# Expert weights kept in float32 and loaded in place, with the expert bias added by VectorE

## The reference, cut to what matters

```python
xk = x_prev + (x - x_prev) * tmk            # xv, xr likewise
k = xk @ Wk.T + bk; v = xv @ Wv.T + bv; r = xr @ Wr.T + br
rwkv = sigmoid(r) * wkv_scan(k, v, time_decay, time_first)
x1 = layernorm(x + rwkv @ Wo.T + bo)

logits = x1 @ wg                            # 8 experts
idx = argmax(softmax(logits)); gate = probs[idx]
y = gate * (x1 @ W[idx].T + b[idx])
out = layernorm(x1 + y)
```

## Time and profile before

| | |
|---|---|
| time of the runs | 700.25 us median of 3 (700.14 to 702.02) |
| profiled execution, its own time | 702.84 us |
| its span, first to last instruction | 701.0 us, mean granted TensorE clock 0.927 |
| TensorE matmul (PE) busy | 600.3 us (86%) |
| VectorE (DVE) busy | 570.2 us (81%) |
| ScalarE (ACT) busy | 374.9 us (53%) |
| GpSimd (POOL) busy | 321.8 us (46%) |
| blocks and last rows / routing / expert loop | about 0 to 506 / 506 to 540 / 540 to 701 us |

### The profile page before, as it was taken

One profiled execution on the slowest core, in us unless ns is written; L12 is line 12 of the kernel. 1 busy time (PEld: TensorE's weight loads), 2 busy tenths in 40 slices (PEclk: granted clock), 3 DMA queues, 4 the chain that ended last, 5 costly groups with the idle time before them and its releaser, 6 DMA issues. The chain is left out here.

```text
span 701.0 us, 8827 instructions
## 1 busy us (share of the span) xinstructions
PE 600.3 (86%) x2521; PEld 447.4 (64%) x2522; DVE 570.2 (81%) x819; ACT 374.9 (53%) x656; POOL 321.8 (46%) x257
## 2 busy tenths in 40 slices
PE   0577779999999999999999999798613999999992
PEld 0365656676687677677677677464603777777871
DVE  7959899999999999999999996754697566676762
ACT  3355566477576476576477476442520355555542
POOL 4735444444445435435434431612257466666641
PEclk9889999999999999999999999988655799999996
DMA  8030010041032031031031041053420344444430
GB/s 302 2 120 1 0 61 0 2 150 31 0 122 60 0 120 58 2 107 60 13 106 60 16 165 60 16 168 131 134 106 16 93 141 134 142 140 137 139 119 5
DMA packets 26863, 56.80 MB, mean 81 GB/s; under 512 B 3832, under 2 KB 3832, under 8 KB 26836
## 3 DMA queue, kind: packets, MB, share of 16 engines
q1 hardware_dynamic: 20596, 37.85, 16.3%
q0 software_dynamic: 6240, 18.62, 8.3%
HBM read 39.64 MB, written 18.61 MB: 83 GB/s over the span
## 5 line engine op out<-in xcount | busy, mean ns | idle before, releaser
L916 POOL TENSOR_TENSOR mixed<-unsplit,mixed 128x1024 fp32r<-128x1024 f32 x44 | 104.5, 2394 | 133.7 <-ACT mixed L637 133.7
L434 PE MATMUL kb<-mixed,w_kvr 128*128 128x512 f32 x384 | 98.8, 408 | 24.4 <-DVE mixed L1289 16.7
L434 PE MATMUL vb<-mixed,w_kvr 128*128 128x512 f32 x384 | 102.1, 417 | 14.9 <-DVE evn L1104 9.2
L610 PE MATMUL y_ps<-w_e,xgT 128*128 x468 | 114.8, 394 | 0.0
L434 PE MATMUL rb<-mixed,w_kvr 128*128 128x512 f32 x384 | 102.9, 418 | 9.0 <-DVE ee L1118 7.7
L434 PEld LDWEIGHTS kb<-mixed,w_kvr 128*128 128x128 f32 x384 | 74.2, 197 | 42.7 <-issue 16.3
L452 PE MATMUL y_ps<-w_o,rw 128*128 128x512 f32 x224 | 100.8, 593 | 0.0
L610 PEld LDWEIGHTS y_ps<-w_e,xgT 128*128 128x128 f32 x468 | 88.7, 190 | 18.1
L434 PEld LDWEIGHTS vb<-mixed,w_kvr 128*128 128x128 f32 x384 | 74.4, 198 | 36.1 <-DVE evn L1104 12.0
L434 PEld LDWEIGHTS rb<-mixed,w_kvr 128*128 128x128 f32 x384 | 74.1, 195 | 31.7 <-DVE ee L1118 9.0
L1055 DVE SCALAR_TENSOR_TENSOR unsplit<-diff,vec,xb 128x512 f32<-128x512 f32 x96 | 74.2, 834 | 8.1 <-PE kb L434 6.0
(11 more groups left out here) (178 smaller groups left out, 1024.4 us busy)
## 6 DMA issues: line engine op xcount, KB each, us to landing
rows<-x SPq DMA_DIRECT2D x32, 256.0 KB, 2.7
x_rows<-rows SPq DMA_DIRECT2D x32, 256.0 KB, 2.1
we_raw<-w_experts SPq DMA_DIRECT2D x8, 1024.0 KB, 6.0
xb<-xT SPq DMA_DIRECT2D x4, 1026.0 KB, 5.3
xb<-xT SPq DMA_DIRECT2D x3, 1024.0 KB, 5.1
w_raw<-w_square SPq DMA_DIRECT2D x2, 1024.0 KB, 9.7
xb<-xT SPq DMA_DIRECT2D x2, 512.0 KB, 5.1
w_raw<-w_square SPq DMA_DIRECT2D x2, 512.0 KB, 6.8
```

Of the source, the lines that this page charges most:

```text
L434: mm = pe.matmul(bank, w_kvr[:, m, a, h, o:o + P], mixed[:, m, bb, h, :], start=(k == 0), stop=(k == 3 * CH - 1))
L610: mm = pe.matmul(y_ps[:, parity, :], xgT[:, third, a, c, :], w_e[:, bass.ds(e, 1), bb, c, :].rearrange("p u o -> p (u o)"), start=False, s ...
L916: pool.tensor_tensor(mixed[:, m, LO, 2 * hp:2 * hp + 2, :], unsplit[:, m, LO, 2 * hp:2 * hp + 2, :], mixed[:, m, HI, 2 * hp:2 * hp + 2, :] ...
```

## The change

- The experts' matrices stay float32 and are loaded straight into their final place (`load_experts`); the raw buffers, `expert_hi` and `expert_lo` are gone. `w_e` takes half the space. The buffers of the weights and mixed inputs of K, V and R are placed one by one, so that experts 0 to 3 can be loaded when block 7's last K projection is done, experts 4 to 7 after its last V projection, and the biases (`b_all`, one copy per partition, 2 MB in all) after its last R projection.
- The expert matmuls are four float32 ones per tile instead of 12 in fp32r; the transposed tile is copied once by ScalarE (`move_gathered`), with no low part.
- The bias is no matmul any more. VectorE adds gate x bias to the gathered row before the product is there (`add_bias`, two tiles ahead), with a register load of the expert number on VectorE, and `add_gathered` adds gate x product to that. The selector `sel_e`, `bias_rows`, `part` and `part8` are gone.
- Block 7's rows have their own buffer (`rows_last`), loaded as soon as the last mixed inputs are formed; their stores come last on SyncE's queue.
- The wait of VectorE for the stores of all rows (L1389) is gone; GpSimd's own wait for them before its first gather stays.
- The lines of VectorE that compute the gates stand, in both kernels, between the one-hot table that TensorE counts and the wait for the counts; ScalarE has no expert copies left around its exponential for them.

```diff
-            def load_expert(q):
-                wait(sp, we_lo[q % 2], q // 2)
-                sp.dma_start(we_raw[q % 2][:], we_v[EXPERT_ORDER[q]]).then_inc(we_loaded[q % 2], 16)
+            def load_experts(experts):
+                for e in experts:
+                    sp.dma_start(w_e[:, e], we_v[e]).then_inc(we_loaded, 16)
...
                     sp.wait_ge(mixed_f32, BLOCKS * 6)
-                    load_expert(0)
-                    load_expert(1)
+                    for j in range(TPB):
+                        sp.dma_start(rows_last[:, j], x_v[i * TPB + j]).then_inc(last_loaded, 16)
...
+                if s.last:
+                    sp.wait_ge(k_filled, CHUNKS)
+                    load_experts(range(EXPERTS // 2))
...
+            sp.wait_ge(v_filled, CHUNKS)
+            load_experts(range(EXPERTS // 2, EXPERTS))
+            sp.wait_ge(r_filled, CHUNKS)
+            sp.dma_start(b_all[:].rearrange("p e o -> p (e o)"),
+                         b_experts.rearrange("e o -> (e o)").partition_broadcast(P)).then_inc(biases_loaded, 16)
             store_rows(BLOCKS - 2, (2, 3))
+            for j in range(TPB):
+                sp.wait_ge(x1_ready, (BLOCKS - 1) * TPB + (j + 1))
+                sp.dma_start(x1_v[(BLOCKS - 1) * TPB + j], rows_last[:, j]).then_inc(row_stored[j], 16)
...
                 e = pe.value_load(tile_ei[0:1, bass.ds(k, 1)], min_val=0, max_val=EXPERTS - 1)
-                pe.wait_ge(turned_lo, k + 1)
-                pe.wait_ge(sel_set, k + 1)
+                pe.wait_ge(turned_moved, k + 1)
                 pe.wait_ge(y_taken, k + (TILES + 1))
-                pe.matmul(y_ps[:, parity, :], sel_e[:, third, :], bias_rows[:], start=True, stop=False)
                 for c in range(CH):
-                    for a, bb in ((HI, HI), (HI, LO), (LO, HI)):
-                        mm = pe.matmul(y_ps[:, parity, :], xgT[:, third, a, c, :],
-                                       w_e[:, bass.ds(e, 1), bb, c, :].rearrange("p u o -> p (u o)"),
-                                       start=False, stop=(c == CH - 1 and (a, bb) == (LO, HI)))
+                    mm = pe.matmul(y_ps[:, parity, :], xgT[:, third, c, :],
+                                   w_e[:, bass.ds(e, 1), c, :].rearrange("p u o -> p (u o)"),
+                                   start=(c == 0), stop=(c == CH - 1))
...
-                act.activation(xgT[:, n % 3, HI], turned_ps[n % 2], ACT.Copy).then_inc(turned_hi, 1)
+                act.activation(xgT[:, n % 3], turned_ps[n % 2], ACT.Copy).then_inc(turned_moved, 1)
...
-            for j in range(TPB):
-                dve.wait_ge(row_stored[j], BLOCKS * 16)
...
-            expert_lo(dve, 7)
+            dve.wait_ge(tiles_ready, 1)
...
+            def add_bias(k, r, n):
+                dve.wait_ge(gathered[n], r * 16 + 16)
+                wait(dve, scattered[n], r * 16)
+                e = dve.value_load(tile_ei[0:1, bass.ds(k, 1)], min_val=0, max_val=EXPERTS - 1)
+                dve.scalar_tensor_tensor(out=yo[:, n], in0=b_all[:, bass.ds(e, 1), :].rearrange("p u o -> p (u o)"),
+                                         scalar=gates[:, bass.ds(k, 1)], in1=xg[:, n],
+                                         op0=ALU.mult, op1=ALU.add).then_inc(bias_added, 1)
+
-            def add_gathered(k, r, n):
+            def add_gathered(k, n):
                 dve.wait_ge(expert_filled, k + 1)
-                wait(dve, scattered[n], r * 16)
+                dve.wait_ge(bias_added, k + 1)
                 dve.scalar_tensor_tensor(out=yo[:, n], in0=y_ps[:, n % 2, :], scalar=gates[:, bass.ds(k, 1)],
-                                         in1=xg[:, n], op0=ALU.mult, op1=ALU.add).then_inc(y_taken, 1)
+                                         in1=yo[:, n], op0=ALU.mult, op1=ALU.add).then_inc(y_taken, 1)
```

More of the change, by code:

```diff
@@ L159, in build @@
         cap27 = place("cap27", [P, 1], F32)
-        part = place("part", [P, 1], F32)
-        part8 = place("part8", [P, 1], F32)
         behind = place("behind", [P, P], F32R)
@@ L594, in turn @@
                 pe.wait_ge(gathered[n], r * 16 + 16)
-                wait(pe, turned_lo, k - 1)
+                wait(pe, turned_moved, k - 1)
                 for c in range(CH):
@@ L616, in _ @@
             pe.wait_ge(ids_ready, 1)
-            for n in range(2):
-                pe.wait_ge(we_lo[n], EXPERTS // 2)
+            pe.wait_ge(we_loaded, EXPERTS * 16)
             turn(0, 0, 0)
@@ L775, in step @@
                 reciprocal_guess(i, 0)
-                if s.last:
-                    act.wait_ge(k_filled, CHUNKS)
-                    expert_hi(0)
                 if s.half == 0:
@@ L861, in norm_last @@
                 act.wait_ge(nmr_ready, last * 2 + (j + 1))
-                act.activation(rows[:, j], rows[:, j], ACT.Identity, bias=nmr[:, j:j + 1],
+                act.activation(rows_last[:, j], rows_last[:, j], ACT.Identity, bias=nmr[:, j:j + 1],
                                scale=rstd[:, j:j + 1]).then_inc(x1_ready, 1)
@@ L895, in norm2 @@
                                scale=rstd2[:, n:n + 1]).then_inc(out_ready, 1)
-            for n in range(2):
-                act.wait_ge(we_lo[n], EXPERTS // 2)
             for k in range(3):
-                turned_split_hi(k, k)
+                move_gathered(k, k)
             rounds = (SORTED - 3) // RING
@@ L1318, in _ @@
             for j in range(TPB):
-                add_rows(last, j, y_banks[j])
-                statistics(last, j)
+                dve.wait_ge(last_loaded, TPB * 16)
+                dve.wait_ge(y_filled, last * TPB + (j + 1))
+                dve.tensor_tensor(rows_last[:, j], rows_last[:, j], y_banks[j], ALU.add).then_inc(y_taken, 1)
+                dve.wait_ge(y_taken, last * TPB + (j + 3))
+                dve.bn_stats(bn[:, j, :], rows_last[:, j]).then_inc(bn_done, 1)
                 if j:
@@ L1427, in shift2 @@
                                          op0=ALU.mult, op1=ALU.mult).then_inc(nmr2_ready, 1)
-            for k in range(3):
-                turned_split_lo(k, k)
-            add_gathered(0, 0, 0)
-            rounds = (SORTED - 3) // RING
+            dve.wait_ge(biases_loaded, 16)
+            add_bias(0, 0, 0)
+            add_bias(1, 0, 1)
+            add_gathered(0, 0)
+            rounds = (SORTED - 2) // RING
             def step(r, n):
-                turned_split_lo(r * RING + (n + 3), (n + 3) % RING)
-                shift2(r * RING + n, n)
-                add_gathered(r * RING + (n + 1), r + (n + 1) // RING, (n + 1) % RING)
+                k = r * RING + n
+                add_bias(k + 2, r + (n + 2) // RING, (n + 2) % RING)
+                shift2(k, n)
+                add_gathered(k + 1, (n + 1) % RING)
             for n in range(RING):
```

179 lines of the change are left out of this document (59 added, 120 removed).

## The result

The changed kernel takes 690.82 us (median of 4 runs, 689.75 to 692.61); the kernel before, in the same series, 701.13 us (4 runs, 700.14 to 703.22). The ratio is 0.9847, with a 95% interval of 0.9821 to 0.9873: faster by 10.3 us. The profiled execution took 691.61 us, its span 689.8 us, at a mean granted clock of 0.949.

A forecast was written before the change was run, and what follows sets the result against it. TensorE was taken to bound the expert loop, VectorE the routing. 27.1 us gained before the first gather, less 17.6 us for the float32 product, gave -9.5 us: 690.8 us for the median, range 687 to 699.

The forecast's parts named there:

- a: Block 7's last R projection, 447.4: VectorE's product with the guess unblocked, TensorE at full clock; 5.6 us earlier behind the projection.
- b: Block 7's outputs, 473.1: VectorE's result unblocked, TensorE through with block 6 and the outputs at 480.4, 11.7 us earlier.
- c: Last turns and logits, 490.7: VectorE's shift unblocked; logits end 17.5 us earlier (18.7 at full clock, 15.3 at half).
- d: Routing, 510.1: VectorE's cast of 32 columns no longer blocked by GpSimd, 3.9 us saved.
- e: Routing, 531.1 and 536.8: comparison unblocked, VectorE's own subtraction gone; `ids` then waits for list matmuls, 5.7 us earlier.
- f: Expert product in the loop: float32 matmuls cost 0.45 us more per tile, 17.6 us in all, bounds 16.4 and 21.5.
- g: VectorE in the expert loop: needs 3.0 to 3.5 us of a 4.0 us period, so it waits for the product.
- The rival in which GpSimd holds it: Expert loop: GpSimd's gather and scatter block the bias operation, VectorE needs 4.4 us per tile; 707 us, chance 0.09.
- h: Expert and bias loads end by 500, last rows' stores by 503, first gather about 512: 9 us of cover.

The follow-up runs named there:

- the bias alone: The kernel with subtractions on VectorE and the expert number loaded early, its bias moved from TensorE to VectorE, the product still fp32r: 681.18 us.
- the second experiment: The kernel before, with each of GpSimd's six expert subtractions cut into four of 128x512: 692.44 us, ratio 0.9865.

## Why the prediction was right, and where by luck

- *What bounds it.* Right. The subtractions of GpSimd held VectorE, and the kernel with them moved to VectorE is 21 us faster with the product left alone.
- *a and b.* The projection waits 0.83 us and takes 3.01 (0.8 and 2.7 foretold). TensorE is through with the outputs at 481.5, where I had 480.4; the blocks of this execution run 1.5 us later than those of the old one (`ee` at 448.90, and not at 447.38), so against its own blocks it is on time. The lag is not the change's: it is there in the blocks already (the last first addition to `state` starts at 441.12, before at 439.60), and in two of the variants above with the same blocks as the changed kernel that instruction starts at 439.79 and 439.49.
- *c.* The foretold place of `mx` was 489.0, it came at 489.77: 16.7 us earlier, 18.2 with that lag taken off, close to the 18.7 of full clock. I had taken 17.5.
- *d and e.* From `mx` to `ids` 32.7 us became 23.2: 9.6 less, and 3.9 + 5.7 = 9.6 was foretold. As foretold, `ids` now waits for the list matmuls (0.79 us), and the last of them started 0.06 us behind VectorE's last table instruction.
- *Before the first gather*, in all: 26.3 us earlier (539.93 to 513.66), 27.1 foretold.
- *f.* The mis-sized term. The product is 8 records 0.43 apart, as read from the old trace, but the spacing rose by 0.377 us, not 0.45: 14.3 us and not 17.6, even below my bound of 16.4. Two parts were off, in opposite directions. I kept the turns' gap at the old 0.56, and it is 0.43: the tile without a gap takes 3.87, not 4.00. Why is not shown; it is not the register load, for with that load moved ahead the typical tile of the fp32r kernel still takes 3.40 to 3.45. And of the irregular gaps, 0.12 us per tile in the old kernel, I let the longer product leave 0.03, where 0.07 are left. The Trainium skill (FP8 and Floating Point Precision, "TensorE Precision Notes") has four passes for float32: by it the product would be 3.55 us, an estimate from 16 times the 0.222 of an fp32r matmul; the trace gives 3.44, so 3.87 fp32r matmuls for one float32, and the measurement decides.
- *g.* VectorE waited for the product, 0.4 us per tile of the loop, not the product for it. But "3.0 to 3.5" held only at its upper end, and to give VectorE's new work no price was wrong by 0.1 us per tile, 3.5 us (the run without bias). The bias operation was never above 0.758 us. The rival in which GpSimd holds it didn't come; the reverse did, see below.
- *h.* Loads land more slowly than foretold (below), but all in time: the first gather is issued 0.7 us behind `ids`, and GpSimd doesn't wait for the rows' stores.
- *The sum.* -26.3 + 14.3, and 0.7 us lost at the start of the loop, is -11.3 for the profiled executions, -9.5 foretold. For the medians it is -10.3. That the median fell on the foretold 690.8 is in part luck: f was 3.3 us too dear, the gain ahead of the loop 0.8 us too large and the start of the loop 0.7 us too cheap, and the kernel before ran at 701.13 in this series, 0.9 us above the median that I started from. Without the blocks' lag of 1.5 us, for which no run shows a cause, the foretold 27.1 would have been 0.7 too small instead.

## What to carry to other kernels

Look for instructions of one engine whose length is another's: a 1-column shift of 4 us is not work but a lock, and it can be paid back by cutting or moving the *other* engine's operation. Here the change bought this freedom with a slower product, while moving the same subtractions into VectorE's waits gives the same freedom without one: 680.0 us against 690.8, and 674.7 with the register load ahead of the transposes. In both kernels that load cost TensorE 0.07 to 0.10 us per tile behind four short transposes (0.43 us), and hardly anything behind the product of 2.9 or 3.4 us: it belongs behind the longest work of the queue. And before an operation is moved to an idle engine, ask which wait it will fill, for in the wrong order it doesn't fill one but adds itself to it.

## What the runs showed that was not expected

- *The lock works against GpSimd too.* Its copy of 128 row numbers takes 0.22 us; 5 of the 33 in the loop took 0.70 to 0.79 us, and all five began inside VectorE's bias operation or within 0.01 us of its start. The changed kernel, POOL and then DVE:

```profile
536.74 0.73 POOL L951 COPY id_now<-ids 128x1 uint32 x1
```

```profile
536.68 0.75 DVE L1350 SCALAR_TENSOR_TENSOR yo<-b_all,gates,xg 128x512 f32<-128x512 f32 x1 [0.56 <-issue]
```

  This copy began 0.06 us behind the bias operation and ended 0.04 us behind its end. The gathers are held as well: nine of those in the loop, all begun inside a bias operation, took 1.26 to 1.51 us, where none of the kernel without the bias takes more than 1.17. In the changed kernel these delays seem to cost nothing, for TensorE waits for no gathered row between 530 and 665 us. (With the shift first no copy took more than 0.222 us, but that run has another pace and can't tell.) Where GpSimd is near the pace they do count: see the bias alone, and the first gather of the kernel with the subtractions on VectorE.
- *Part of the lock is left.* In the routing VectorE's four table instructions still run beside GpSimd's four, as the prediction noted without a price:

```profile
501.57 8.98 DVE L1329 TENSOR_TENSOR place_q<-dest_f,iota_q 128x1024 fp32r<-128x1024 f32 x4
```

```profile
500.27 9.20 POOL L943 TENSOR_TENSOR place_list<-place_k,gate_parts 128x640 fp32r<-128x640 f32 x4 [41.29 <-DVE place_k L1323]
```

  The same comparison over 128x1280, ahead of them, takes 1.49 us, so one of 128x1024 would take about 1.2 (an estimate by size). They come every 2.24 us, the pace of GpSimd's: about 4 us of the routing, on the path to `ids`, look like the same turn-taking. No run moved either of the two tables, so it is not shown.
- *Landing is slower when more is asked for at once.* Four expert loads of 1 MB in a row, and again four with the biases behind them (page, DMA issues):

```profile
w_e<-w_experts SPq DMA_DIRECT2D x8, 1024.0 KB, 9.1
...
b_all<-b_experts SPq DMA_DIRECT2D x1, 2048.0 KB, 16.1
```

  The old kernel's, issued one or two at a time, landed in 6.0 us; these took from 5.5 to 13.2. I had used the 6.0 for a queue of four.
- *Cutting a blocking operation is no cure for the lock*, only for its length: the four quarters in the second experiment take 6.94 us beside VectorE, as if each engine had a piece in turn.
